# Delta rule: diagonal blocks placed by VectorE transposes, value tiles in halves, key norms turned first, carry beside far corner

## The reference

```python
q = silu(conv4(h @ Wq)); k = silu(conv4(h @ Wk)); v = silu(conv4(h @ Wv))   # depthwise, causal
gk = -exp(A_log) * softplus(h @ Wgk + dt_bias); beta = sigmoid(h @ Wb + b_b)
q = l2norm(q) * 64 ** -0.5; k = l2norm(k)
for t in tokens:                       # the state S is 64 x 128 for each head
    S = S * exp(g_t)
    delta = (v_t - k_t @ S) * beta_t
    S = S + outer(k_t, delta)
    o_t = q_t @ S
out = (rmsnorm(o) * g_norm_weight * g * sigmoid(g)) @ Wo        # g = h @ Wg
```

## Time and profile before

| | us |
|---|---|
| median of 3 runs | 1688.55 |
| lowest and highest | 1687.41, 1693.38 |
| the profiled execution's own time | 1687.46 |
| its span, first to last instruction | 1685.6 |
| TensorE, VectorE, ScalarE, POOL busy | 1311.7, 924.4, 749.1, 421.7 |
| mean granted TensorE clock | 0.852 |

### The profile page before, as it was taken

The page is one execution under the profiler, slowest core; times in us unless marked ns, Lnnn a source line. Parts: engine busy times, 40 slices in busy tenths (PEclk is TensorE's granted clock), DMA queues, the critical chain, the costliest instruction groups (busy, mean ns, idle before and its releaser), DMA issues. The chain is left out here.

```text
span 1685.6 us, 26913 instructions
## 1 busy us (share of the span) xinstructions
PE 1311.7 (78%) x9629; PEld 916.8 (54%) x9629; DVE 924.4 (55%) x2013; ACT 749.1 (44%) x1356; POOL 421.7 (25%) x438
## 2 busy tenths in 40 slices
PE   6997994567888975677768738695899868697998
PEld 3786453346455642256446527463577646365676
DVE  3687455667665466845854682465333366565111
ACT  2343562331552245854674525373355443163432
POOL 0223000012200027532452501210444435410000
PEclk9899796567798987979969867797899979798999
DMA  6000000100000000000000000420000000000000
GB/s 245 2 0 0 1 1 1 77 1 1 1 2 1 1 1 1 0 2 1 1 1 1 1 1 1 182 99 1 1 1 0 1 1 1 1 2 2 1 1 13
DMA packets 6339, 27.27 MB, mean 16 GB/s; under 512 B 1329, under 2 KB 4433, under 8 KB 5585
## 3 DMA queue, kind: packets, MB, share of 16 engines
q1 hardware_dynamic: 6224, 25.76, 3.9%
HBM read 25.23 MB, written 0.52 MB: 15 GB/s over the span
## 5 line engine op out<-in xcount | busy, mean ns | idle before, releaser
L745 DVE TENSOR_REDUCE L_xattn_top<-banks 128x4 f32<-128x512 f32 x128 | 80.6, 671 | 55.0 <-PE banks L603 55.0
L1188 DVE SCALAR_TENSOR_TENSOR L_ffn_a<-banks,L_ffn_act_out 128x512 f32<-128x512 f32 (+1 forms) x72 | 47.7, 662 | 103.1 <-POOL L_ffn_act_out L1118 103.1
L1118 POOL TENSOR_TENSOR L_ffn_act_out<-L_ffn_act_out,L_ffn_combine 128x512 f32<-128x512 f32 (+1 forms) x72 | 71.6, 994 | 77.6 <-ACT L_ffn_act_out L1164 77.6
L1132 PE MATMUL banks<-region_a,L_ffn_hs 128*128 128x512 f32 x144 | 73.0, 591 | 16.3 <-POOL L_ffn_hs L1111 15.2
L750 DVE TENSOR_TENSOR L_xattn_p<-banks,L_xattn_top 128x512 f32<-128x512 f32 x128 | 82.5, 686 | 5.2 <-issue 0.4
L700 ACT ACTIVATE L_xattn_p<-L_xattn_p 128x512 f32<-128x512 f32 x128 | 75.8, 630 | 18.5 <-DVE L_xattn_p L750 18.4
L492 PE MATMUL banks<-w_const,h 128*128 128x128 f32 x96 | 24.9, 424 | 75.7 <-DVE h L487 75.7
L1164 ACT ACTIVATE L_ffn_act_out<-banks 128x512 f32<-128x512 f32 (+1 forms) x72 | 41.3, 573 | 89.8 <-PE banks L1132 89.8
L708 ACT ACTIVATE L_xattn_pT<-banks 128x512 f32<-128x512 f32 x128 | 69.7, 595 | 19.5 <-PE banks L616 19.5
L603 PE MATMUL banks<-L_xattn_ks,L_xattn_qT 32*128 32x512 f32 x256 | 76.6, 702 | 1.6 <-ACT L_xattn_qT L689 1.6
L2311 PE MATMUL banks<-hT,region_b 128*128 128x512 f32 x96 | 54.6, 706 | 29.1 <-DVE region_a L2705 12.9
(11 more groups left out here) (498 smaller groups left out, 3359.1 us busy)
## 6 DMA issues: line engine op xcount, KB each, us to landing
region_b<-in_L_ffn SPq DMA_DIRECT2D x1, 6216.0 KB, 29.7
region_a<-in_L_ffn SPq DMA_DIRECT2D x1, 4416.0 KB, 13.3
region_b<-in_L_attn SPq DMA_DIRECT2D x1, 3150.5 KB, 10.5
region_a<-in_L_ffn SPq DMA_DIRECT2D x1, 3080.5 KB, 21.1
region_b<-in_L_attn SPq DMA_DIRECT2D x1, 1633.5 KB, 9.1
region_b<-in_L_xattn SPq DMA_DIRECT2D x1, 835.0 KB, 9.6
w_tables<-in_tables SPq DMA_DIRECT2D x1, 832.0 KB, 12.6
region_b<-in_L_ffn SPq DMA_DIRECT2D x1, 768.0 KB, 11.0
```

Of the source, the lines that this page charges most:

```text
L745: nc.vector.tensor_reduce(top[:, i, :], rows_of(score[i][:], 4), X, ALU.max)
L1118: nc.gpsimd.tensor_tensor(rows, rows, bc(combine[:, n, EXPERTS * q:EXPERTS * q + ex], 2, HALF // EXPERTS), ALU.mult).then_inc(weighed, 1)
L1132: nc.tensor.matmul(up[e][:, 0:widths[q]], hs[:, u, :], w["up"][:, up_at[q]:up_at[q] + widths[q]], start=True, stop=True).then_inc(hidden, 1)
```

## The change

- Value tiles leave the list of tiles (`TILES`). Of each group but the first, they are made in eight halves `H` of 512 tokens in one bank each (`project_values`, `scale_values_tap`, `tap_values`, `silu_values`), one half a step.
- In the opening, tile order and owners change (POOL convolves tile 1 alone), and norms are turned in two rounds: the keys' (`r = 0`), then the queries' (`r = 1`). POOL computes the key norms' powers ahead of the fourth square. The same two rounds are used for the later groups.
- VectorE makes blocks 2 and 3 of `blocks_in` by multiplying the key products with the decays again, in place of copying them from AT.
- `place_upper(b)` (VectorE) transposes each diagonal block from PSUM into AT; `upper_c` and ScalarE's `keep_diagonals` are gone. `keep_lower` moves to ScalarE.
- `carry(k)` and `far_corner(k − 1)` are issued head by head next to each other; `carried` gets two buffers.

```diff
     ORDER = (2, 3, 0, 1, 4, 5, 6, 7)
-    FIRST = (2, 4, 3, 0, 5, 1, 6, 7)
-    NORMED_FIRST = (0, 2, 3, 5)
+    FIRST = (2, 4, 3, 0, 1, 5, 6, 7)
     bank, banks = g.bank, g.banks
-    TILES = range(8 * GROUPS)
-    pool_tiles = [M for M in TILES if (M in (1, 4) if M < 8 else M % 8 < 4)]
+    TILES = [M for M in range(8 * GROUPS) if M < 8 or M % 8 < 4]
...
+    def value_half(hg, H):
+        return c[:, 4 + H // 2, 4 * (H % 2):4 * (H % 2) + 4, :]
...
             square_tile(2, first_squares(1))
-            add_taps(4)
             square_tile(3, first_squares(2))
-            square_tile(5, first_squares(3))
             for part in range(4):
                 key_norms(0, part)
+            square_tile(4, first_squares(3))
...
+            def project_values(hg, H):
+                if H == 0:
+                    pe.wait_ge(corner_kept, 2 * hg)
+                    pe.wait_ge(low_kept, 2 * hg)
+                elif H == 1:
+                    pe.wait_ge(upper_ready, 4 * hg)
+                else:
+                    pe.wait_ge(v_convolved, 8 * (hg - 1) + H - 1)
+                nc.tensor.matmul(bank_half[H % 2], value_weights(hg, H)[0], g.hT[:, (H % 2) * HALF:(H % 2 + 1) * HALF],
+                                 start=True, stop=True).then_inc(v_proj, 1)
...
-                if n % 4 == 0:
-                    pe.wait_ge(low_kept, 2 * hg + n // 4 + 1)
-                if n == 0 and hg + 1 < GROUPS:
-                    tile_read(pe, B * hg + B + 2)
+                if carries:
+                    if n % 4 == 0:
+                        pe.wait_ge(low_kept, 2 * hg + n // 4 + 1)
+                    if n == 0:
+                        pe.wait_ge(lower_kept, 2 * hg + 2)
+                        if hg + 1 < GROUPS:
+                            tile_read(pe, B * hg + B + 2)
+                    after(pe, carry_kept, k)
+                if corners:
+                    m = n - 1 if carries else B - 1
+                    if m == 0:
+                        pe.wait_ge(upper_ready, 4 * hg + 4)
+                    if m % 4 == 0:
+                        pe.wait_ge(corner_kept, 2 * hg + m // 4 + 1)
+                    pe.wait_ge(carry_kept, B * hg + m + 1)
                 for h in range(G):
-                    last = nc.tensor.matmul(bank_carry[64:128, 64 * h:64 * h + 64], AT[0:64, n, h, 64:128],
-                                            half_inverse[0:64, n, h, :], start=True, stop=True)
-                last.then_inc(carry_made, 1)
-
-            def far_corner(k):
-                n, hg = k % B, k // B
-                if n == 0:
-                    pe.wait_ge(diag_kept, hg + 1)
-                if n % 4 == 0:
-                    pe.wait_ge(corner_kept, 2 * hg + n // 4 + 1)
-                pe.wait_ge(carry_kept, k + 1)
-                for h in range(G):
-                    last = nc.tensor.matmul(bank_carry[0:64, 64 * h:64 * h + 64], carried[64:128, h, :],
-                                            AT[64:128, n, h, 64:128], start=True, stop=True)
-                last.then_inc(far_made, 1)
+                    if carries:
+                        to = nc.tensor.matmul(bank_carry[64:128, 64 * h:64 * h + 64], AT[0:64, n, h, 64:128],
+                                              half_inverse[0:64, n, h, :], start=True, stop=True)
+                    if corners:
+                        far = nc.tensor.matmul(bank_carry[0:64, 64 * h:64 * h + 64], carried[64:128, m % 2, h, :],
+                                               AT[64:128, m, h, 64:128], start=True, stop=True)
+                if carries:
+                    to.then_inc(carry_made, 1)
+                if corners:
+                    far.then_inc(far_made, 1)
...
-                tile_norms(0, m)
-            turn_norms(0)
+            project(2)
+            project(3)
+            project(4)
+            tile_norms(0, 0)
+            tile_norms(0, 1)
+            turn_norms(0, 0)
+            project(5)
+            project(6)
+            tile_norms(0, 2)
+            tile_norms(0, 3)
+            turn_norms(0, 1)
+            project(7)
...
-                    if more and s < B and s % 2 == 0:
-                        project(first + B + 4 + s // 2)
+                    if s <= B:
+                        carry_beside_far_corner(k if s < B else k - 1, s < B, s > 0)
+                    if more and s < B:
+                        project_values(hg + 1, s)
                     if 1 <= s <= B:
                         solve_values(k - 1)
-                    if s < B:
-                        far_corner(k)
+                    if more and s in (0, 1, 4, 5):
+                        tile_norms(hg + 1, (0, 1, None, None, 2, 3)[s])
+                    if more and s in (2, 6):
+                        turn_norms(hg + 1, s // 4)
                     if s >= 2:
                         turn_outputs(k - 2)
                     if 1 <= s <= B:
                         outputs(k - 1)
...
-            def keep_diagonals():
-                for b in range(4):
-                    last = nc.scalar.activation(AT[BLOCKS[b], :, :, BLOCKS[b]].rearrange("p b h t -> p t (b h)"),
-                                                upper_c[BLOCKS[b], :, :], ACT.Copy)
-                last.then_inc(diag_kept, 1)
+            def keep_lower(hg, b):
+                act.wait_ge(lower_ready, hg + 1)
+                after(act, carry_made, B * hg)
+                nc.scalar.activation(half_inverse[BLOCKS[b], :, :, BLOCKS[b]].rearrange("p b h s -> p (b h) s"),
+                                     lower_c[BLOCKS[b], :, :].rearrange("p s q -> p q s"), ACT.Copy).then_inc(lower_kept, 1)
...
                 keep_corners(hg, 0)
-                keep_diagonals()
                 keep_corners(hg, 1)
-                if more:
-                    silu(first + B + 3)
                 for s in range(B + 2):
                     k = first + s
+                    if 1 <= s <= B:
+                        keep_far(k - 1)
                     if s < B:
                         keep_carry(k)
+                    if more and s == 0:
+                        silu(first + B + 3)
+                    if more and s < B:
+                        scale_values_tap(hg + 1, s)
                     if 1 <= s <= B:
                         keep_z(k - 1)
-                    if s < B:
-                        keep_far(k)
+                    if more and s in (2, 6):
+                        keep_norms_T(hg + 1, s // 4)
                     if s >= 2:
                         keep_yT(k - 2)
-                    if more and s < B and s % 2 == 0:
-                        scale_taps(first + B + 4 + s // 2)
+                    if more and s >= 2:
+                        silu_values(hg + 1, s - 2)
                     if 1 <= s <= B:
                         square(k - 1)
-                    if more and s >= 2 and s % 2 == 0 and s <= B:
-                        silu(first + B + 4 + (s - 2) // 2)
-                    if more and s == 4:
-                        keep_norms_T(hg + 1)
...
                                         ALU.mult).then_inc(a_ready, 1)
                 nc.vector.tensor_tensor(by_parity(PT[:, n, :, :]), decayed(k, 0), by_parity(dec[:, u, :, :]),
-                                        ALU.mult).then_inc(p_ready, 1)
-
-            def keep_blocks(k):
-                n = k % B
-                dve.drain()
+                                        ALU.mult)
                 if n == 0:
                     dve.wait_ge(normed, 4 * (k // B) + 4)
                 for b in (2, 3):
-                    nc.vector.tensor_copy(blocks_in[BLOCKS[b], :, G * n:G * n + G].rearrange("p t h -> p h t"),
-                                          AT[BLOCKS[b], n, :, BLOCKS[b]])
+                    for_pairs = blocks_in[BLOCKS[b], :, G * n:G * n + G].rearrange("p t (j e) -> p e j t", e=2)
+                    last = nc.vector.tensor_tensor(for_pairs, decayed(k, 1)[BLOCKS[b], :, :, BLOCKS[b]],
+                                                   by_parity(dec[BLOCKS[b], u, :, BLOCKS[b]]), ALU.mult)
+                last.then_inc(p_ready, 1)
...
                 nc.vector.transpose(lower_c, solve.rearrange("p t s -> p s t")).then_inc(lower_ready, 1)
-                nc.vector.transpose(upper_c, solve).then_inc(upper_ready, 1)
+
+            def place_upper(b):
+                nc.vector.transpose(AT[BLOCKS[b], :, :, BLOCKS[b]].rearrange("p b h t -> p t (b h)"),
+                                    solve[BLOCKS[b], :, :]).then_inc(upper_ready, 1)
...
-                for i in range(3):
-                    tap(m, i)
-            keep_norms(0)
+            for i in range(3):
+                tap(4, i)
+            keep_norms(0, 0)
+            key_norms(0)
+            for i in range(3):
+                tap(5, i)
+            for i in range(3):
+                tap(6, i)
...
                 first, more = B * hg, hg + 1 < GROUPS
                 coefficients(hg)
```

(22 more changed lines are left out.)

168 lines of the change are left out of this document (89 added, 79 removed).

## The result

The changed kernel takes 1663.35 us (median of 4 runs, 1663.06 to 1664.79) against 1689.43 for the kernel before measured beside it (4 runs, 1687.41 to 1693.38). The ratio is 0.9845, with a 95% interval of 0.9832 to 0.9859: faster by 1.5%. The profiled span fell from 1685.6 to 1661.6 us, by 24.0. The forecast was 1657, with a range of 1640 to 1672: the direction and range hold, but the stage itself gave 19 us where the sum said 31, as the table shows.

The account below looks back on a forecast made before the run. Each phase has its own limit: VectorE in chunk loop and inversion, ScalarE's block copies in corners, waits for VectorE's last tap in the output loop. 1687.5 + 7 − 15 − 15 − 8 = 1656.5, said as 1657 us; range 1640 to 1672.

Parts of the forecast that it names:

- Opening: Stage start to first scaling: the powers delay the fourth square, its sum, turn and project(7); +7, range +2 to +7.5.
- Chunk loop: Chunk loops: two products from PSUM at 0.25 each replace two copies; about −5 a group, −15 in all.
- two-chunk loop: Chunk loop: keys(k) through the products to keys(k+2) takes 5.4 us for two chunks; 2.75 a chunk taken.
- Rival A: Chunk loop: block products no cheaper than the copies, VectorE keeps 3.7 a chunk; 1672 us, chance 0.08.
- Corners: First transpose to first square: four ScalarE copies (7.81 us) ahead of the second corner go; −15, range −20 to −9.
- rival B: Corners: place_upper's strided transposes take 1.95 us, pushing corners by 1.2 three times; 1661 us, chance 0.12.
- Pairing: Corners: carry and far corner, issued together, take little more than one of them; 1.1 us at the low level.
- Output loop: Output loops of groups 0 and 1: half tiles, one per step, 6.15 us a step; −4 each, −8.
- G: Chunk loop: TensorE, busy all the time, has its clock fall, making the kernel slower; chance 0.03.
- D: Whole stage: opening +2, 2.56 a chunk, corners −20, output loop 5.6 a step; 1635 us, chance 0.10.
- F: Opening: its loss eats the gain; together with rivals A and C it would leave 1680 us, chance 0.03.
- C: Output loop: six waits of half tiles cost what one long wait did, no gain; 1665 us, chance 0.12.

Follow-up runs that it names:

- s1: Changed kernel with POOL's fourth square of the opening ahead of the four key-norm powers instead of behind them; 1652.31 us.
- s7: Changed kernel with the fourth square first, and project(7), its scaling and its taps ahead of the second round of norms; 1654.27 us.
- s5: Changed kernel with ScalarE's keep_norms_T ahead of keep_z in steps 2 and 6 of the output loop; 1659.93 us.
- s2: Changed kernel with the two block products made copies from AT again, one chunk behind, as in the kernel before; 1670.39 us.
- s3: Changed kernel with place_upper's transposes and the block products writing packed instead of strided, so values are not the kernel's; 1656.35 us.
- s8: Changed kernel with the placing undone: one 128-partition transpose into a scratch tile, and four ScalarE copies into AT between the corners; 1673.75 us.
- s4: Changed kernel with all of a step's carry matmuls issued first and the far-corner matmuls behind them, not in turns; 1663.76 us.
- s6: Changed kernel with the halves of the value tiles going round three PSUM banks instead of two; 1651.67 us.

## Why the prediction was right, and where not

- **Opening (+7, came +9.7).** The chain is the forecast's; s1 and s7 take it apart link by link. The 2.7 beyond it go with TensorE's low level in the first projections (s5); the forecast's times come from one execution, which had them at 5.19 and 5.40. My upper end of +7.5 was too near for that reason.
- **Chunk loop (−15, came −11.0).** Mechanism right (s2: the products alone), price wrong: I took 0.25 a block product from a product of 108 packed elements; it is 0.38, of which 0.09 is the stride (s3). The rest I had no ground for: 128 elements can't be put below the 0.27 of 108, and packed they take 0.29. At 0.38 VectorE's own work is 2.89 a chunk and not the two-chunk loop's 2.75. Rival A, no gain, is false; what it saw in the 1.56 is what the copies lose beside POOL, and the products don't lose it.
- **Corners (−15, came −14.7).** Right in the sum and in its parts (21.3, 22.3, 20.5 against 22, 22, 19.6), and s8 gives 13.9 back. The sum stands by offsets as well: the sentence that a transpose takes 1.2 was wrong, it takes 1.91, as rival B had it, and 1.24 with packed writes (s3). But B charged 1.2 a group for it and it cost less: TensorE's corners waited 0.88 for VectorE, and the first carry came 12.4 after the transpose where 11.6 was forecast, +0.8. In group 0 the clock gave more than that back (solve_values in 1.05), in group 2, without it, the corner is 0.9 above the forecast. The sign “no ScalarE copies of 1.95” was written too widely: keep_lower's two take 1.94 to 2.00, now on ScalarE.
- **Pairing.** The taking of the pair at little more than one of them holds: in turns eight and eight matmuls take 1.05 at the low level, with one bank for both. Each record of a carry starts within 0.01 of one of a far corner, though both write that bank (870.99 and 870.99, 871.25 and 871.26 in group 1). Yet I charged a wrong alternative: unpaired doesn't mean 2.2 but 1.5 (s4), since the matmuls overlap anyway.
- **Output loop (−8, came −1.9).** The step of the forecast that failed by most. The loop through the last half tap was there, but mis-sized: 6.34 for a bare step where 6.15 stood. A half tap takes 0.74 and not 0.66, half of a whole one, which is 0.08 of it; the other 0.1 isn't traced to a term. A norm sum costs 0.33 where I wrote 0.25. And in the first step of groups 0 and 1 (8.95 and 9.20 where 7.15 follows from the terms) the wait of 1.9 for the taps was followed by a projection at TensorE's low level. s6 shows that it hangs on the two banks: with a third the wait, the low level behind it and the 6.34 all go.
- **The rivals.** A and G are false (the loops gained 11.0, at a clock of 0.98 to 1.00). No run has a chunk loop at the low level, so what it would cost isn't shown. B is right in its price and small in its effect. D (1635: an opening of +2, 2.56 a chunk, corners of −20, 5.6 a step) is false in each of its terms, and F needed A. C, no shorter output loop, comes nearest to what happened: seven steps at a mean of 6.8 and 6.9 are its sign (6.9), and its time (1665) is nearer than mine, by luck in so far as the 4.9 outside the stage are in it. Its mechanism, waits of half tiles that cost what one long wait did, holds only with two banks.
- **The sum.** The stage gave 12 us less than forecast: 2.7 in the opening, 4.0 in the chunk loops, 0.3 in the corners, 6.1 in the output loops, less 1.3 at the ends of groups. The −4.9 outside the stage were in no term: 1.6 are chance, 3.3 are not explained. Without them the result would have been some 1668, still inside the range. That 1663 lies so near 1657 is in part luck; the stage alone gave three fifths of the forecast.

## What to carry to other kernels

When an edit halves a piece of work and doubles how often it is waited for, cost the whole step with its fixed parts, and ask whether one more buffer would end the wait: a third bank was worth 15.7 us here, where the split alone gave 1.6 in the same two groups. On an engine with a queue, look at what a long instruction that nobody needs yet (four powers, 6.45 us; four copies, 7.81) is standing in front of. When short instructions of one kind take two or three different times, look at what the other engines do beside them. Where the clock moves, compare phases and not spans.
